# Delta rule links on one Trainium2 core: three 32-column products per head for the blocks below the diagonal, in place of one product over all blocks

## The reference, cut to what matters

```python
def delta_rule(q, k, v, beta):
    def step(W, inp):
        qt, kt, vt, bt = inp
        wk = jnp.einsum('bhde,bhe->bhd', W, kt)
        v_new = bt * (vt - wk)
        W = W + jnp.einsum('bhd,bhe->bhde', v_new, kt)
        out = jnp.einsum('bhde,bhe->bhd', W, qt)
        return (W, out)
```

## Time and profile before

| what | value |
|---|---|
| median of 3 runs | 2385.87 us (2373.57 to 2449.76) |
| the profiled execution, its own time | 2385.36 us |
| its span | 2383.6 us |
| PE busy, weight loads busy | 1922.0 us (81%), 1270.6 us (53%) |
| DVE, ACT, POOL busy | 1461.9 us (61%), 1020.8 us (43%), 1126.5 us (47%) |
| mean granted TensorE clock | 0.879 |

### The profile page before, as it was taken

The page is one execution under the profiler, slowest core; times in us unless marked ns, Lnnn a source line. Parts: engine busy times, 40 slices in busy tenths (PEclk is TensorE's granted clock), DMA queues, the critical chain, the costliest instruction groups (busy, mean ns, idle before and its releaser), DMA issues. The chain is left out here.

```text
span 2383.6 us, 39549 instructions
## 1 busy us (share of the span) xinstructions
PE 1922.0 (81%) x14130; PEld 1270.6 (53%) x14130; DVE 1461.9 (61%) x2714; ACT 1020.8 (43%) x2368; POOL 1126.5 (47%) x1101
## 2 busy tenths in 40 slices
PE   7977799999987487947657777599987699975991
PEld 4544587878876367944212224266653466643550
DVE  4658866655500331223889896699978799965552
ACT  3652244444432102412756565555547455551110
POOL 3111834555450140032169991399971699935005
PEclk9998899999997557978779999599998799996995
DMA  7001111111110006821022220122210222201662
GB/s 289 1 1 21 39 37 28 29 37 22 37 31 19 7 28 171 224 69 28 3 60 86 75 72 2 30 78 72 74 43 3 56 76 72 74 21 57 192 186 66
DMA packets 196265, 149.77 MB, mean 63 GB/s; under 512 B 93363, under 2 KB 155403, under 8 KB 194554
## 3 DMA queue, kind: packets, MB, share of 16 engines
q1 hardware_dynamic: 191482, 138.61, 20.6%
q0 software_dynamic: 4608, 8.86, 1.3%
HBM read 108.80 MB, written 39.19 MB: 62 GB/s over the span
## 5 line engine op out<-in xcount | busy, mean ns | idle before, releaser
L1628 POOL TENSOR_TENSOR mc_hc<-mc_states,mc_c_sb 128x1024 f32<-128x1024 f32 x192 | 451.2, 2350 | 62.7 <-DVE mc_states L1718 50.5
L1718 DVE TENSOR_TENSOR_SCAN mc_states<-psum,mc_dbu 128x512 f32<-128x512 f32 x384 | 459.5, 1217 | 13.7 <-ACT psum L1639 6.4
L1756 PE MATMUL psum<-mc_hc,ident 128*128 128x512 f32 x768 | 412.1, 633 | 51.4 <-POOL mc_hc L1628 51.4
L1639 ACT ACTIVATE psum<-dt,a 128x508 f32<-128x508 f32 x384 | 261.3, 686 | 18.8 <-DVE mc_states L1718 17.9
L787 POOL TENSOR_TENSOR fw_tmp<-zeros 128x30 f32<-128x30 f32 (+14 forms) x240 | 125.3, 522 | 257.0 <-DMA zeros<-fw_blocks 238.8
L1618 POOL TENSOR_TENSOR mc_dbu<-dtu,mc_b_sb 128x384 f32<-128x384 f32 x192 | 191.3, 997 | 13.6 <-ACT mc_b_sb L1646 13.6
L1756 PEld LDWEIGHTS psum<-mc_hc,ident 128*128 128x128 f32 x768 | 123.8, 192 | 117.6 <-POOL mc_hc L1628 73.1
L1704 DVE TENSOR_TENSOR mc_dbu<-psum,dtu 128x640 f32<-128x640 f32 x192 | 153.9, 801 | 7.3 <-PE psum L1733 7.0
L791 POOL TENSOR_TENSOR zeros<-zeros,fw_tmp 128x30 f32<-128x30 f32 (+14 forms) x240 | 130.0, 542 | 18.8
L1646 ACT ACTIVATE mc_b_sb<-psum 128x192 f32<-128x192 f32 x192 | 63.5, 331 | 167.9 <-PE psum L1739 167.4
L824 ACT ACTIVATE fw_U<-psum 32x512 f32<-32x512 f32 x128 | 75.4, 589 | 135.0 <-PE psum L1071 79.6
(11 more groups left out here) (434 smaller groups left out, 4175.3 us busy)
## 6 DMA issues: line engine op xcount, KB each, us to landing
mc_c_sb<-c_rows SPq DMA_DIRECT2D x192, 256.0 KB, 3.1
e_w<-in_L_ffn_ew SPq DMA_DIRECT2D x64, 256.0 KB, 3.2
slots_x<-zeros SPq DMA_DIRECT2D x12, 1024.0 KB, 14.3
e_x<-slots_x SPq DMA_DIRECT2D x96, 128.0 KB, 2.3
slots_y<-e_y SPq DMA_DIRECT2D x96, 128.0 KB, 2.0
e_w<-in_L_ffn_w SPq DMA_DIRECT2D x64, 128.0 KB, 2.2
fw_blocks<-fw_A SPq DMA_DIRECT2D x128, 32.0 KB, 1.7
zeros<-fw_blocks SPq DMA_DIRECT2D x8, 512.0 KB, 3.7
```

The source lines that it names most:

```text
L1628: nc.gpsimd.tensor_tensor(hc[:, k % 2], states[:, k % 2], c_sb[:, k % AHEAD, :].unsqueeze(1).to_broadcast([P, HALVES, GT]), ALU.mult).then ...
L1639: nc.scalar.activation(decay4[:, f, :, 1:P], z["dt"][:, f, cols].rearrange("p (b t) -> p b t", b=GS)[:, :, 1:P], ACT.Exp, scale=z["a"][:, ...
L1718: nc.vector.tensor_tensor_scan(out=states[:, k % 2, f, :], data0=decay_ps[:, f, :], data1=dbu[:, k % 2, f, :], initial=0.0, op0=ALU.mult, ...
L1756: last = nc.tensor.matmul(y_ps[:, f, :], m.ident, hc[:, k % 2, f, :], start=False, stop=(n == NSTATE - 1), skip_group_check=True)
```

## The change

Three things are changed. `links` makes, in place of one product over 128 rows and 128 columns per head, three products per head, for i = 1, 2, 3: rows 32i to 32i+31 of A, columns 0 to 32i-1 of A (the stationary operand, so 32, 64 or 96 columns), and the 32 columns of the inverse of block i as the moving operand. The loop over i is outside the one over the four heads. Since nothing outside the diagonal blocks of XT is read any more, `XT` shrinks to 32 columns per head, the loads into it become contiguous, and its zeroing by POOL falls away, with the second count that SP waits for.

```diff
@@ delta_rule_stage
-        XT = sb("XT", [P, SLOTS, H, P])
+        XT = sb("XT", [P, SLOTS, H, BLK])
...
-                sp.wait_ge(s["zeroed"], 2)
+                sp.wait_ge(s["zeroed"], 1)
...
-                            sp.dma_start(XT[BLK * i:BLK * (i + 1), j % SLOTS, :, BLK * i:BLK * (i + 1)],
+                            sp.dma_start(XT[BLK * i:BLK * (i + 1), j % SLOTS, :, :],
                                          inverses[j, i].rearrange("h b a -> b h a")).then_inc(xt_in[j % SLOTS], 16)
...
                 nc.gpsimd.memset(eps[:, :], EPS).then_inc(s["zeroed"], 1)
-                nc.gpsimd.memset(XT[:, :, :, :], 0.0).then_inc(s["zeroed"], 1)
...
-                    for h in range(HH * half, HH * (half + 1)):
-                        last = nc.tensor.matmul(BT4[:, h % HH, :], A[:, j % LAG, h, :], XT[:, j % SLOTS, h, :], start=True, stop=True)
+                    for i in range(1, NB):
+                        rows = slice(BLK * i, BLK * (i + 1))
+                        for h in range(HH * half, HH * (half + 1)):
+                            last = nc.tensor.matmul(BT4[0:BLK * i, h % HH, rows], A[rows, j % LAG, h, 0:BLK * i], XT[rows, j % SLOTS, h, :],
+                                                    start=True, stop=True)
                     last.then_inc(s["bt_mm"], 1)
...
-                            last = nc.tensor.matmul(RU8[rows, h, :], XT[rows, j % SLOTS, h, rows], vb[rows, j % LAG, h, :], start=(h == 0),
+                            last = nc.tensor.matmul(RU8[rows, h, :], XT[rows, j % SLOTS, h, :], vb[rows, j % LAG, h, :], start=(h == 0),
```

## The result

The changed kernel takes 2491.47 us (median of 4 runs, 2476.80 to 2535.08) against 2388.26 us for the kernel before, a ratio of 1.043 with a 95% interval of 1.0335 to 1.0525. That is slower, as forecast, but by 103 us where 50 were forecast, and outside the range of 2400 to 2458. Most of that difference lies outside the stage of the change: what follows the stage takes 1604 us in the profile of the kernel before, and 1638 in that of `after_again`, whose series has a median of 2428.13.

What follows compares the result with a forecast made beforehand. PE was taken to bound the stage. Full-turn links +34.0, tail links +15.8, tail clock +12, filled wait -9.1 and its low clock -3 gave +49.7 on 2385.36, so 2435 us; range 2400 to 2458, the forecast's own 2422 to 2448.

Steps and rivals of the forecast that it cites:

- PE bounds the full turns, and what is added to it is added to the time: Up to 640 us PE is busy 40.00 of 40 us, so work added to its turns lengthens the time.
- Pace of a pass: In the links the weight load paces a pass: 0.028, 0.055 and 0.083 us for 32, 64 and 96 stationary columns.
- Change of shape: Four changes per links half, two of them inner, at 0.09 us each; a half of 1.77 us against 0.98.
- Rival 1: No cost between the three new link shapes: +0.5 us per half, +29 us, 2414 us; chance 0.18.
- Rival 2, products side by side: Narrow link products overlap on different array rows, a half of 0.87 us: 2388 us, not slower; chance 0.12.
- The buffer, the loads, the zeroing: 0: Dropping POOL's zeroing is worth 0 (ends 0 and -3.5); contiguous loads into XT taken as 0 (ends -2 and +2).
- The wait for the last inverses is filled: -9.1 us: PE's 9.12 us wait for the last group's inverses is filled by longer links: -9.1 us (ends 0 and -9.1).
- The clock in the tail: 25 us more at the lower clock, +12 us (ends 0 and +35); the low clock after the filled wait goes, -3.
- The price of a us at the lower level: 0.48: In a tail turn, 2.9 us lost for 6 us at 1.2 GHz, so 0.48 us per us there.
- In full turns the clock stays at 1.00: Before 640 us the granted clock stays full despite thin links, so the sum has no clock cost there.
- the covered wait: A 0.8 us wait behind `links(1)` in the first full-clock turn covers as much of the added links: 34.8 becomes 34.0.
- rival 3: Heavier: 96 columns load like 128 (+14), or the clock falls through the tail (+23) or in full turns: 2452 to 2475; chance 0.17.

Runs made afterwards that it cites:

- after_again: The changed kernel unchanged, run and profiled once more in the series of the follow-up runs: ratio 1.0426 to the kernel before.
- heads_outer: The changed kernel with the link loops exchanged, heads outside and block rows inside, so each product changes shape: 2661.43 us against 2383.53, 1.117 in one run.
- full_only: The kernel before, with its buffer, loads and zeroing, and the three narrow products only for items 0 to 21 (full turns): ratio 1.0216.
- tail_only: The kernel before, with its buffer, loads and zeroing, and the three narrow products only for items 22 to 31 (the tail): ratio 1.0223.
- thin: The kernel before with one product per head and full weight loads, streaming 32 columns instead of 128 for every item but the first; output wrong: ratio 1.0160.
- warm_thin: `thin` plus two unused products of 256 columns per tail turn, where PE waits for ACT's copy of a block row: ratio 0.9981.
- warm_after4: The changed kernel plus four unused products per tail turn: 256 columns behind block rows 1 and 2, 512 ahead of the first links, 256 behind the second: ratio 1.0339.
- warm_after: The changed kernel plus two unused products of 256 columns per tail turn, behind block rows 1 and 2: ratio 1.0433.
- tail_both: The kernel before, with the narrow products made first and the four full ones over them for items 22 to 31: ratio 1.0244.
- n96: The kernel before with its one product per head cut to 96 columns of A and the last 96 of XT, over all 128 rows: ratio 0.9972.
- warm_before: The kernel before plus two unused products of 256 columns per tail turn, in the waits for ACT's copies: ratio 0.9981.

## Why the prediction was wrong

- *PE bounds the full turns, and what is added to it is added to the time.* Right. Full turns without a fall of the clock grew by 1.67 us, twice the growth of a half.
- *Pace of a pass.* Right but for 2 to 3 ns: 31, 58 and 85 ns against 28, 55 and 83 forecast. 96 columns lie where the line between 64 and 128 puts them. The Trainium skill ("TensorE: Matmul & The Clock Gate", "LDWEIGHTS (loading the stationary operand)") has a load go by its columns, and by that rule, which gives 80 ns for 96 columns, the trace agrees but for the few ns that all three paces have above it.
- *Change of shape.* Right in size and in number: 89 ns at each joint, the two inner ones included, which no row of before could show. Rival 1 is out. The Trainium skill ("TensorEngine Tiling (Array Packing)", "Key Properties") says that a change of tiling mode drains the engine; the 120 and 147 ns at the joints, against paces of 31 and 58, agree. In place of the 28 ns that the forecast added to each group there are 22. With the slightly longer paces a half came to 1.82 us, forecast 1.77, which makes the links 53.4 us in all (32 x 1.67) against 50.6.
- *Rival 2, products side by side.* Out for this kernel. Neither the changed kernel nor `heads_outer`, whose neighbours lie on different rows, shows any overlap across shapes.
- *The buffer, the loads, the zeroing: 0.* Right within the intervals, by `full_only` and `tail_only`.
- *The wait for the last inverses is filled: -9.1 us.* Right, it is gone.
- *The clock in the tail: +12 us from 25 us more at the lower level, and -3 behind the filled wait.* Wrong, and this is the term that sank the forecast. In turns 32 to 41 the lower level took 119 us and not 38: 82 us more. Of the 41.6 us that these turns grew, the links are 16.7 and the filled wait -9.1. The rest is 34 us, where the forecast had 12 - 3 = 9.
- *The price of a us at the lower level: 0.48.* Nearly right: 34 us for 82 is 0.41. The forecast divided 2.9 us by the 6 us of a stretch that it had cut out; the fall in that turn lasted 6.8 us, from 747.9 to 754.7, which gives 0.43.
- *In full turns the clock stays at 1.00.* Wrong too, and the sum had no term for it: turns 11 to 31 had 41.8 us at the lower level. They grew by 53.9 us, of which 21 pairs of links are 35.1 and the covered wait -0.8, so some 20 us stand beside the fall of the clock. I had this only as the heavier half of rival 3, held against by the block rows and `right_side` being thin without a fall.

Together the stage's 98 us are 53.4 of links, -9.1 and -0.8 of waits, 53.6 that go with the lower clock, and 1 at the ends. Against the 49.7 forecast, 45 of the 48 missing us are the clock's and 3 the links'.

The step that failed was a number without rows behind it: I saw that the clock fell after block rows with waits and rose in links, `read_out` and `output`, saw that the change makes two of those four blocks narrow, and then took 25 us for it in the tail and nothing in the full turns. In hindsight a tail that already fell for 38 us was a warning. A change that makes half of its full-width blocks narrow should have been given the whole tail, the end of +35 that stood in the text, which is close to the 34 us measured, and the full turns a term of their own.

What stays open: which combination of narrow work and waits lets the clock fall was not isolated. `thin` and `warm_thin` show that the clock makes the time where the links are no longer, and `warm_after4` shows it in part for the changed kernel itself. `warm_after` and the profile of `tail_both` show that neither idle products nor full ones hold the clock up by their mere presence.

## What to carry to other kernels

Where few columns are streamed, a product costs its weight load, by stationary columns and whatever the number of rows (31, 58 and 85 ns a pass for 32, 64 and 96 columns of 32 rows here, 85 for 96 columns of 128 rows). Each change of tile shape costs another 0.11 us at full clock. Cutting away useless blocks pays only if the passes get shorter in both directions and no change of shape is added, as in `n96`. Before thinning PE's work, look at the granted clock of the stretch: if it already falls there, thinner work can keep it down, and that cost as much again here as the new instructions (54 us beside 53). In waits that can't be removed, unused full-width products can be worth their place; in `warm_before` they gave 0.2%, in `warm_after` nothing.

## What the runs showed of the hardware that was not expected

- A stretch of PE where nothing but the number of streamed columns shrank, with loads and passes the same, went from 0.85 (644 to 769 us before) to 0.54 granted clock, and a turn from 10.06 to 16.91 us (`thin`).
- Idle products of 256 columns, one in each of two waits of 0.68 us, held the clock at 1.00 in eight of the nine turns 33 to 41, at no cost in the turn (`warm_before`, 10.06 us). Without them it falls in six of the nine. The one that falls with them is the turn with the wait for the last inverses.
- The same idle products can also fail: between narrow links the clock fell all the same, at the lower clock they no longer fit into the waits, and `warm_after` had turns of 19.95 us beside ones of 15.4, where `after_again` has 17.07.
